# A transformer layer with routed experts: where the residual is kept and added

## What is computed

```
x = x + xattn(layernorm(x), ctx)          # 16 heads of 8, softmax over 120 keys, Wo, bo
n = layernorm(x)
probs = softmax(n @ Wr.T)                 # 8 experts
topv, topi = top_k(probs, 2)
x = x + sum over the 2 picked experts e of topv_e * (gelu(n @ W1[e] + b1[e]) @ W2[e] + b2[e])
```

## Time and profile before

| what | value |
|---|---|
| runs | 1073.62 us median of 3 (1069.72 to 1073.95) |
| profiled execution, its own time | 1068.32 us |
| its span, first to last instruction | 1066.5 us |
| mean granted TensorE clock | 0.927 |
| busy: PE, DVE, ACT, POOL | 78%, 73%, 51%, 46% |
| DMA packets, bytes moved | 154,718, 138.82 MB |

### The profile page before, as it was taken

One profiled execution on the slowest core, in us unless ns is written; L12 is line 12 of the kernel. 1 busy time (PEld: TensorE's weight loads), 2 busy tenths in 40 slices (PEclk: granted clock), 3 DMA queues, 4 the chain that ended last, 5 costly groups with the idle time before them and its releaser, 6 DMA issues.

```text
span 1066.5 us, 23998 instructions
## 1 busy us (share of the span) xinstructions
PE 827.1 (78%) x5926; PEld 581.7 (55%) x5926; DVE 779.1 (73%) x2536; ACT 539.4 (51%) x1001; POOL 487.8 (46%) x705
## 2 busy tenths in 40 slices
PE   0587989898989989898998878148988898988700
PEld 0455666665656666565666554036666676766500
DVE  8865888888888888888888876626665656565535
ACT  1143555455555545455555443037767676767500
POOL 6222334343433435343343553704666666767620
PEclk9998999999999999999999896569999999999955
DMA  1244324233332423233232454365656666656359
GB/s 46 53 112 131 86 74 103 63 97 79 91 86 72 105 60 100 76 96 82 75 102 68 138 147 131 134 205 183 218 192 221 188 213 200 213 182 209 105 162 310
DMA packets 154718, 138.82 MB, mean 130 GB/s; under 512 B 25742, under 2 KB 122363, under 8 KB 153660
## 3 DMA queue, kind: packets, MB, share of 16 engines
q1 hardware_dynamic: 137148, 117.15, 38.8%
q0 software_dynamic: 9088, 17.07, 4.6%
q10 hardware_dynamic: 8448, 4.20, 1.3%
HBM read 72.61 MB, written 33.92 MB: 100 GB/s over the span
## 4 chain that ended last, share of the span: by engine, by line
PE 35%; DVE 22%; issue 15%; DMA 12%; SPq 6%; POOL 5%; ACT 3%; DVEq 1%; POOLq 1%; ACTq 0%
DVE mx L606 6%; PE bank L1148 5%; POOL yd L536 4%; DMA b2tile<-bsb 4%; PE bank L1158 4%; PE bank L1138 3%; DVE vyy L623 3%; PE bank L1098 3%; PE bank L1121 2%; PE bank L1100 2%; PE bank L1099 2%; DMA wsp<-yd 2%; DMA kb<-ks 2%; PE bank L1262 1%; DVE rows L709 1%
## 5 line engine op out<-in xcount | busy, mean ns | idle before, releaser
L536 POOL DMA_INDIRECT yd<-vs,idn x156 | 163.8, 1050 | 103.7 <-DVE vs L914 66.3
L504 POOL DMA_INDIRECT xd<-rows,posi x128 | 126.2, 986 | 159.5 <-DVE posi L685 123.8
L969 ACT ACTIVATE pt<-bank 120x512 f32<-120x512 f32 x256 | 145.6, 596 | 104.3 <-PE bank L1148 103.6
L894 DVE TENSOR_TENSOR qb<-hid,qb 128x512 fp32r<-128x512 f32 x156 | 108.1, 693 | 113.9 <-ACT hid L1054 113.6
L606 DVE TENSOR_REDUCE mx<-bank 128x4 f32<-128x480 f32 x256 | 161.2, 652 | 11.0 <-PE bank L1138 11.0
L1051 ACT ACTIVATE qb<-bank,b1tile 128x512 fp32r<-128x512 f32 x156 | 107.5, 689 | 76.4 <-PE bank L1313 70.3
L1138 PE MATMUL bank<-kb,qs 128*128 128x480 f32 x256 | 103.0, 447 | 46.9 <-DVE mx L606 35.5
L1148 PE MATMUL bank<-qb,ks 128*120 128x512 f32 x256 | 122.2, 498 | 6.9 <-DMA qb<-negm 6.7
L1158 PE MATMUL bank<-pt,vs 120*32 120x128 f32 x2048 | 113.2, 294 | 3.5 <-ACT pt L969 1.6
L1054 ACT ACTIVATE hid<-bank,b1tile 128x512 f32<-128x512 f32 x156 | 106.4, 682 | 0.0
L1138 PEld LDWEIGHTS bank<-kb,qs 128*128 128x128 f32 x256 | 48.0, 197 | 88.2 <-DVE mx L606 67.8
(11 more groups left out here) (192 smaller groups left out, 2046.4 us busy)
## 6 DMA issues: line engine op xcount, KB each, us to landing
kb<-wd SPq DMA_DIRECT2D x78, 512.0 KB, 5.0
qb<-qs SPq DMA_DIRECT2D x128, 128.0 KB, 2.4
kb<-ks SPq DMA_DIRECT2D x128, 120.0 KB
rows<-xd SPq DMA_DIRECT2D x39, 264.0 KB, 2.7
wd<-wsp SPq DMA_DIRECT2D x8, 1024.0 KB, 4.9
xres<-in_x SPq DMA_DIRECT2D x32, 128.0 KB, 2.2
hid<-in_L_ffn_W SPq DMA_DIRECT2D x16, 256.0 KB, 5.3
pt<-yd SPq DMA_DIRECT2D x16, 256.0 KB, 5.8
```

Source lines behind the costliest of these rows:

```text
L504: g.indirect_dma_start(xd, bass.IndirectOffsetOnAxis(ap=posi[r.parity][:, bk:bk + 1], axis=0), rows[r.parity][:, bk // 2, bk % 2, :], None ...
L536: g.indirect_dma_start(yd, bass.IndirectOffsetOnAxis(ap=idn[k][:, j:j + 1], axis=0), yrow[k][:, j, :], None, bounds_check=2 * NTOK - 1, oo ...
L894: v.tensor_tensor(hhl[:, 1, c, :], hid[:, c % 2, :], hhl[:, 0, c, :], ALU.subtract).then_inc(h_lo, 1)
L969: a.activation(pt[t % NP][:].rearrange("p j q -> p (j q)"), scores[t % 2][0:KL, :], ACT.Exp, scale=SCALE).then_inc(exp_done, 1)
```

## The change

- A DRAM tensor `acc` with 8,192 rows and 512 spare rows takes the place of `yd`. In each slot SP stores the finished residual of chunk s-1 from `xres` to `acc`. This store waits for `x1_done` and stands behind the mask row and ahead of `load_x`.
- Both picks of a token have the token's own index. The expert scatters add to `acc` (`compute_op=ALU.add`). Before a tile's scatters POOL waits for those of the previous tile.
- Rows that fill up a tile carry the index of one of the 512 spare rows, where zeros are added, instead of NOWHERE.
- The loads of `yd`, DVE's additions and ACT's stores at the end are gone. One DMA from SP's queue copies 8,192 rows of `acc` to the output, DRAM to DRAM.

```
-        yd = nc.dram_tensor("yd", (2 * NTOK, D), F32, kind="Internal").ap()
+        acc = nc.dram_tensor("acc", (NTOK + TB, D), F32, kind="Internal").ap()
...
+            sp.dma_start(acc[NTOK:NTOK + TB, :].rearrange("(p n) w -> p n w", p=P), zrows[:, :, 0:D]).then_inc(acc_zero, 16)
...
+                if exists(n, -1):
+                    m = s + -1
+                    alone(sp, x1_done, s.count(2))
+                    sp.dma_start(acc[bass.ds(m.count(N2), N2), :].rearrange("(b s) d -> s b d", b=2),
+                                 xres[:, bass.ds(m.count(2), 2), :]).then_inc(acc_in, 16)
                 if exists(n, 4):
...
+            sp.wait_ge(acc_in, 16 * NCH)
+            sp.wait_ge(acc_zero, 16)
...
-            for k in range(NY):
-                load_y(k, k)
-            with sp.Fori(0, NQ // NY - 1) as it:
-                for k in range(NY):
-                    sp.wait_ge(fin_b, it * NY + (k + 1))
-                    load_y(k, it * NY + (k + NY))
+            sp.dma_start(out.rearrange("b s d -> (b s d)").rearrange("(p n) -> p n", p=P),
+                         acc[0:NTOK, :].rearrange("t d -> (t d)").rearrange("(p n) -> p n", p=P)).then_inc(out_done, 16)
+            sp.wait_ge(out_done, 16)
...
-            g.memset(zrows[:, :, D:D + 1].bitcast(I32), NOWHERE).then_inc(zrow_done, 1)
+            g.iota(zrows[:, :, D:D + 1].bitcast(I32).rearrange("p n a -> p (n a)"), [[1, TN]], base=NTOK, channel_multiplier=TN).then_inc(zrow_done, 1)
...
-            g.iota(idf[:, :], [[S, 2], [NTOK, 2]], base=0, channel_multiplier=1, allow_small_or_imprecise_dtypes=True).then_inc(kept, 1)
+            g.iota(idf[:, :], [[S, 2], [0, 2]], base=0, channel_multiplier=1, allow_small_or_imprecise_dtypes=True).then_inc(kept, 1)
...
                     alone(pool, idn_done, p.count(1, 1))
+                    if n is None or n >= 2:
+                        alone(pool, y_out[1 - k], (p + -1).uses(64))
                     alone(pool, yr_taken, p.count(1, 1))
                     for j in range(TN):
-                        g.indirect_dma_start(yd, bass.IndirectOffsetOnAxis(ap=idn[k][:, j:j + 1], axis=0), yrow[k][:, j, :], None,
-                                             bounds_check=2 * NTOK - 1, oob_is_err=False).then_inc(y_out[k], 16)
+                        g.indirect_dma_start(acc, bass.IndirectOffsetOnAxis(ap=idn[k][:, j:j + 1], axis=0), yrow[k][:, j, :], None,
+                                             bounds_check=NTOK + TB - 1, oob_is_err=True, compute_op=ALU.add).then_inc(y_out[k], 16)
...
-            def combine(k, it):
...
-            with act.Fori(0, NQ) as q:
...
```

More of the change, by code:

```diff
@@ L65, in moe_attention @@
     NOWHERE = 1 << 20
-    NQ = B // TN
     SCALE = float(DH) ** -0.5
@@ L186, in moe_attention @@
         yrow = [vs_all[0][:, k].rearrange("p h r -> p (h r)").rearrange("p (n d) -> p n d", n=TN) for k in range(2)]
-        NY = 4
-        wflat = flat(wsp, "p k w n").bitcast(F32).rearrange("p (k b d) -> p k b d", k=NY, b=TN)
-        yin = [pt_all, [wflat[:, k] for k in range(NY)]]
         bank = [st.enter_context(nc.psum_tensor(f"bank{k}", [P, 512], F32)) for k in range(8)]
@@ L228, in moe_attention @@
         yt_full, yt_taken, yr_full, yr_taken = sem("yt_full"), sem("yt_taken"), sem("yr_full"), sem("yr_taken")
-        y_in, fin_a, fin_b = [sem(f"y_in{k}") for k in range(4)], sem("fin_a"), sem("fin_b")
+        acc_zero, acc_in = sem("acc_zero"), sem("acc_in")
         xd = nc.dram_tensor("xd", (SPARE + TB, ROW), F32, kind="Internal").ap()
-        yd = nc.dram_tensor("yd", (2 * NTOK, D), F32, kind="Internal").ap()
+        acc = nc.dram_tensor("acc", (NTOK + TB, D), F32, kind="Internal").ap()
         wd = nc.dram_tensor("wd", (E, P, 4 * HID), F32R, kind="Internal").ap()
```

## The result

The changed kernel takes 1202.0 us (median of 4 runs, 1200.2 to 1206.3) against 1071.7 us for the kernel before on the same chip: ratio 1.122, 95% interval 1.120 to 1.125. That is 130 us slower, 52 us more than forecast and 2 us beyond the upper end of the range.

A forecast was written before the change was run, and what follows sets the result against it. Bounds taken: DVE and PE handing work over in attention, POOL's scatter ring in the expert stage, full DMA engines at the end. 1068.3 + 62 + 2.6 + 35 − 18 = 1150 us, range 1085 to 1200.

The forecast's parts named there:

- Attention: Attention slots: SP's store waits for the residual addition, delaying kb copies and query product 2.4 us in 26 slots, 62 us.
- transfers directly ahead of the copies: Attention, SP's queue: three 128 KB transfers directly ahead of the kb copies, so 5.0 us from first issue to product.
- Experts: Expert stage: adding scatters and the wait for the previous tile make 8.5 us per tile, 35 us more.
- The ring that I set up: Expert tiles, new wait: 4.05 first to fourth scatter, 3.6 landing, 0.86 restart, 8.5 us per tile.
- My upper bound of 9.6 us per tile: Expert stage: the addition costs at most one more 2.1 us round in the landing, 78 us in all.
- That ring paces the stage: Expert stage before: scatters, POOL's index copies, DVE's scaling and the next scatter set 7.62 us per tile.
- The end: Kernel's end: one DRAM-to-DRAM copy takes 23.1 us in place of 41.2, 18 us gained (12 to 25).
- Free edits: Prologue's store of zeros hidden behind weight preparation; iota for memset and another constant under 0.1 us each.
- B: SP's wait binds in attention, but the adding scatter lands as today: 1115 us, chance 0.20.
- D: Attention delay absorbed in the slot, adding scatters still cost 35 us: 1088 us, chance 0.10.
- C: Expert stage: adding scatters are the bound, each landing in 5.9 us, 10.8 per tile: 1239 us, chance 0.12.
- E: Early-landing kb copies make SP's attention delay disappear, and adding scatters land as today: 1053 us, chance 0.08.

The follow-up runs named there:

- store_only: Kernel before plus only SP's store of the residual, with its wait for x1, to a DRAM tensor of its own: 1133.6 us, ratio 1.059.
- store_late: Changed kernel with SP's store of the residual moved behind the kb and qb copies of its slot: 1138.6 us, ratio 1.066.
- store_older_chunk: Changed kernel with the store at its place but of the chunk one slot older, so issued without waiting: 1136.1 us, ratio 1.062.
- plain_scatter: Changed kernel with scatters that write instead of add, wait and spare rows kept, sums left out: 1117.4 us, ratio 1.046.
- two_halves_no_wait: Changed kernel, filling rows skipped, picks added to two halves of acc without POOL's wait, second picks left out of the output: 1211.9 us, ratio 1.068, other chip.
- copies_between: Kernel before with POOL's index copies for the next tile between the second and third scatter: 1130.9 against 1135.9 us, ratio 0.995.
- copies_on_dve: Kernel before with the four small copies per tile moved from POOL to DVE: 1041.1 against 1070.5 us, ratio 0.973.
- padding_skipped: Changed kernel with filling rows given an out-of-bounds index again, so skipped: 1234.4 us on the other chip, ratio 1.088, tiles 10.01 us.
- wait_only: Kernel before with only POOL's wait for the previous tile's scatters added: 1141.4 against 1135.9 us, ratio 1.006.
- add_into_output: Changed kernel storing the one-slot-older chunk and adding rows straight in the output, filling rows skipped, no final copy: 1121.6 us, ratio 1.048.

## Why the prediction was wrong

- **Attention: right in mechanism; the size in part by luck.** Forecast 2.4 us per slot and 64.6 in all; measured 2.44 (21.07 − 18.63) and 65.3. store_only reproduces it alone, store_late and store_older_chunk take it away. The copies started 2.4 us behind the end of the addition (forecast 2.05), and the product 4.48 us behind them (forecast 5.0): the two errors nearly cancel. From the end of the `ks` subtractions to the product, a slot has 7.37 us on average instead of 5.28, so the wait itself delays by 2.1 us, not 2.4. The other 0.3 us lie between the product and the next `ks` (13.71 instead of 13.41), where PE in most slots now runs for some us at the lower clock; the forecast had no term for the clock, and no run separates its price. What I had supposed on transfers directly ahead of the copies isn't seen.
- **Experts: the step that failed.** In "from first to fourth start is 3.9 to 4.2 us, I take 4.05" I kept the plain scatter's time on POOL, and charged the addition to the landing alone. Measured is 5.83, and these 1.8 us more than account for the 1.5 that the tiles are above the forecast of 8.5. The ring that I set up holds, with other numbers: 5.83 + 3.19 for the landing + 1.03 to start again = 10.05 (forecast 4.05 + 3.6 + 0.86; the last scatter shows 3.24 for the landing, from 1181.91 to 1185.15). That my landing was close is luck in part: I had put an addition's whole cost there. My upper bound of 9.6 us per tile covered no increase on POOL at all, though the busy time of the scatters' line on POOL was in the profile; had I let it double at most (0.97 more in each of three intervals: 4.05 + 2.9 + 3.6 + 0.86 = 11.4 us), the range would have held 1202 easily. It was also narrower than its own terms: their upper ends add up to 1068 + 78 + 3 + 78 − 12 = 1215. Even so the stage cost 94.5 us (91.6 + 2.9), beyond the 78 that I allowed.
- **How the 2.41 us per tile divide.** plain_scatter: wait and spare rows 0.24 without the addition. two_halves_no_wait: 1.7 of the addition without the wait (9.32 against 7.62 on the other chip). They enhance each other: with plain scatters the ring of the wait is hardly longer than the others of 7.6 us, with adding ones it is 0.7 us longer than they are. In the sum: 92 us, of which 82 need the addition ((10.03 − 7.86) × 38).
- **"That ring paces the stage".** Wrong for the ring that I named, right that POOL's list paces. copies_between cut the named ring and gained 0.5%; copies_on_dve cut also the one through SP's row loads, and gained 2.7%. For the forecast it made no difference, as the new ring is longer than both.
- **The end: right in mechanism, low in size.** 16.1 us instead of 23.1: the copy landed after 15.6 us. With 2.1 us of latency that leaves 4.19 MB in 13.5 us, an estimate of 311 GB/s, my lower end (each byte counted once). The Trainium skill (DMA: Bandwidth & Descriptors, "Anatomy of one DMA — SWDGE (gpsimd) path") has a fit that gives an estimate of 11.6 us for such a size; it is for DMAs issued from GpSimd, and this copy, issued from SP, needed 4 us more. The same fit has no term for adding, and the expert stage contradicts what followed from it (no cost): its estimate of 2.15 us for 64 KB stands against 2.2 to 3.0 for the fourth plain scatters and 3.19 for an adding one, and POOL's own time isn't in it.
- **Free edits.** The first kb issue is at 41.11 us as before, so nothing of the prologue's store shows (in all the runs it lies between 38.7 and 43.5). padding_skipped finds nothing in the spare rows.
- **Rivals.** B and D fall, each by one of the two waits. C had the place right (adding scatters pace the stage) and put the cost in the wrong part, the landing (5.9 us; measured 3.2); its sign, tiles above 10 us, came true without its reason. E falls.

What stays open: why an adding scatter takes POOL 0.58 us longer. It comes together with (26,560 − 9,088) / 156 = 112 more packets per scatter, but no run here separates the two. Nor is it known why the one chip needs 2 us more per attention slot; in wait_only's timeline they lie ahead of the query product, which starts 7.15 us behind the copies' issue on average instead of 5.19, released by DVE's `qs`. That would leave room for late copies, and fits with SP's wait costing less there.

## What to carry to other kernels

A wait put into an in-order queue costs what stands behind it, not what it guards: the store needed a finished residual, the copies behind it didn't; storing data that is one step older, at the same place, was free. Before an operation moves from an engine to the DMA, ask what the issuing engine pays per instruction as well as how the transfer lands, and bound both. And where an engine that is two thirds busy (POOL, 81 of 120 us in the earlier trace rows) paces a stage, look for each signal that other engines get only from the end of its list: taking such small signals elsewhere was worth 29 us here, more than the 25 that the changed end gave.

## What the hardware showed unexpectedly

- An indirect scatter of 128 rows of 512 bytes keeps POOL 0.97 us when it writes and 1.55 when it adds; and in packets the queue has 26,560 instead of 9,088, 112 more per scatter, whether filling rows are written (the changed kernel) or skipped (padding_skipped).
- It takes 1.55 us also where no row is in bounds: the last, spare tile of add_into_output (0 GB/s from 1110 to 1121 us), in the timeline:

```profile
1114.18 1.55 POOL L527 DMA_INDIRECT out<-vs,idn  x1 [0.30 <-issue]
```

- A copy of 4.19 MB from DRAM to DRAM (landed in 15.6 us) runs at about the rate (estimated 311 GB/s) at which the old end moved data between DRAM and SBUF (307 in the earlier trace rows), although it touches DRAM twice.
- After some 2 us of idleness in each slot PE's granted clock was 0.50 for the next stretch of the slot shown (406.4 to 412 us); without SP's wait the stage has 1.00 (store_late), with it 0.91.
- The kernel before differs by 6% between two chips (1070 and 1136 us). In wait_only, 57 us of the difference lie before the first scatter (787 against 730).
